# One Trainium2 kernel, four graph blocks: three pieces of work change places on ScalarE and VectorE

## The chip, the cores and the metric

The kernel runs on one core of a Trainium2 chip. Its time is the device time of one execution in microseconds; the kernel before takes 1280.2 us as the median of three runs (1279.27 to 1281.15). Less is better. The engines are TensorE (PE in the profile, its weight loads PEld), VectorE (DVE), ScalarE (ACT), GpSimd (POOL) and SyncE (SP), which here issues every DMA.

## The reference

For each of 32 graphs with 256 nodes and 256 features (`x`, a weighted adjacency `adj` 256x256, a node mask) four blocks follow each other, each added to its input and layer-normalized:

```python
x = _layernorm(x + _L0_gnn_ref(x, adj, L0_gnn_W))      # relu([x, adj @ x / deg] @ W.T)
x = _layernorm(x + _L1_gnn_ref(x, adj, W1, b1, W2, b2, W3, b3))  # three GCN layers
x = _layernorm(x + _L2_gnn_ref(x, nodemask, adj, adj, W_qkv, W_out, b_out))
x = _layernorm(x + _L3_gnn_ref(x, adj, W_qk, W_v))
```

The third block is attention with 8 heads of 64; the softmax is mixed with `adj` and `exp(-adj)` before it multiplies the values. The last block is a gate: `w = softmax over the nodes of sum(scores * adj)`, and its result is `w * v`. All of it is in float32.

## The kernel before

The kernel has no scheduler: for each engine the order of work is written out by hand as a list of calls, `first_graphs()`, then `slot(s)` in a loop (`FIRST, LAST = 5, G + 1`, 28 slots), then `last_graphs()`. Each engine runs its list strictly in that order; between engines there are only semaphores. A slot works on several graphs at once, each at another stage, so the numbers s - 2, s - 4, s - 6 in the calls are graphs. The same moment has another s on each engine (VectorE's s is ScalarE's s plus 2).

Most products are made of float32r parts: ScalarE copies a result out of PSUM as its high part (`..._h`, line 429), VectorE subtracts that from the result for the low part (`..._l`, line 900), and TensorE multiplies high by high and high by low in one stretch (HI) and low by high in a second (LO). So TensorE waits twice for each operand, for ScalarE and then for VectorE.

The work around the change, with the names of the profile:

- Attention runs over four pairs of heads. `scores(g, p, i)` (VectorE, line 1092) takes the scores of pair p out of PSUM, masks them and finds the row minimum; each call is two reductions. `exps` (ScalarE, line 578) makes the exponentials. `out_hi(g, p)` and `out_lo(g, p)` split a pair's output into `oT_h` and `oT_l`.
- `degrees(g)` on ScalarE (line 482) sums the rows of `adj`; VectorE uses the sums much later.
- The GCN: `gcn_out` (VectorE, line 1071) adds the third layer's product to `x1_b3`, giving `x2_pre`. Behind it `sup0_lo` makes the low part of the next graph's first product, for which TensorE waits in `aggregate(g, LO)` (line 1626, the product `psum<-sup_l,adjT_h`). Then come the normalization `norm_stats`, `norm_mean`, `norm_apply` and TensorE's `x2_transpose`.
- The gate: `tail_gate` makes `minus_gate`, a column of 256 numbers. SyncE turns it into a row by a DMA (`gate_row`); `gate_maximum`, `gate_exps` and `gate_probs` make the softmax on that row, and SyncE turns the row back into a column by a second DMA (`gate_col<-gate_prob`). `tail_out` (VectorE, line 1187) forms the gated sum `x4_pre = qkv3 * gate_col + x3` and waits for that DMA:

```python
if g < DMA_GATE:                                   # DMA_GATE = G - 3
    dve.wait_ge(dma_gate_col, 16 * once(g))
```

- SyncE's list, for k from 2 on, where `load(k)` issues xT, adjT, adj, x (256 KB each) and the mask row of graph k:

```python
if 0 <= k - 5 < DMA_GATE:
    turn_gate(k - 5)
if live(k):
    load(k)
if 0 <= k - 5 < DMA_GATE:
    turn_gate_probs(k - 5)
```

`load(k)` first waits until the buffers of graph k - 2 are free. The last of these in time is ScalarE's `mask_bias(k - 2)` (`minus_big`, line 501). `turn_gate_probs` issues `gate_col<-gate_prob`.

Of the kernel before, what the change touches and what calls it, by code (L numbers as in the profile page):

```python
# [13 lines left out]
def graph_blocks_kernel(nc, x_d, adj_d, nodemask, xT_d, adjT_d, w0_d, w123_d, L1_b1, L1_b2, L1_b3, wqkv_d, wout_d,  # L14
# [22 lines left out]
    with ctx:  # L37
# [200 lines left out]
        def live(g):  # L238
            return 0 <= g < G

        def loaded(g):
            return 16 * (g // 2 + 1)
# [184 lines left out]
        def _(act):  # L427
            def copy(dst, src, scale=1.0):
                return nc.scalar.activation(dst, src, ACT.Copy, scale=scale)  # L429
# [34 lines left out]
            def x_hi(g):  # L464
                if not live(g):
                    return
                act.wait_ge(dma_xT[g % 2], loaded(g))
                copy(fT_of(g)[0][:, :, :], xT_sb[:, g % 2]).then_inc(act_xT, 1)
# [7 lines left out]
            def degrees(g):  # L476
                if not live(g):
                    return
                act.wait_ge(dma_adj[g % 2], loaded(g))
                reuse(act, dve_rdeg, once(g - 1))  # L480
                for t in range(NT):
                    last = nc.scalar.activation(adj_junk[:, t], adj_sb[:, g % 2, t], ACT.Copy,
                                                accum_out=deg[:, t:t + 1])
                last.then_inc(act_deg, 1)
# [104 lines left out]
            def out_hi(g, p):  # L589
                if not live(g):  # L590
                    return
                act.wait_ge(pe_pv, nth(g, p))
                copy(oT[0][:, p], bank(PV[p])[:, 0:N]).then_inc(act_oT, 1)
# [41 lines left out]
            def slot(s):  # L635
                probs_t(s - 3, 2, 0)
                probs_t(s - 3, 2, 1)
                hidden(0, s - 1)
                hidden_hi(0, s - 1)
                probs_t(s - 3, 3, 0)  # L640
                probs_t(s - 3, 3, 1)
                out_hi(s - 3, 2)
                x_hi(s)
                degrees(s)
                exps(s - 2, 0, 0)
                out_hi(s - 3, 3)
                sup_hi(1, s - 1)
                exps(s - 2, 0, 1)
                qk_hi(s - 2, 2)
                gate_exps(s - 4)  # L650
                exps(s - 2, 1, 0)
                hidden(1, s - 1)
                hidden_hi(1, s - 1)
                adj_exp(s)
                exps(s - 2, 1, 1)
                mask_bias(s - 1)
                adj_hi(s)
                norm_apply(3, s - 5)
                sup_hi(2, s - 1)
                sup0_hi(s)  # L660
                values(s - 2)
                self_copy(s)
                qk_hi(s - 2, 3)
                probs_t(s - 2, 0, 0)
                probs_t(s - 2, 0, 1)
                probs_t(s - 2, 1, 0)
                probs_t(s - 2, 1, 1)
                x2_hi(s - 1)
                norm_apply(2, s - 3)
                exps(s - 2, 2, 0)  # L670
                exps(s - 2, 2, 1)
                out_hi(s - 2, 0)
                x3_hi(s - 3)
                x1_hi(s)
                exps(s - 2, 3, 0)
                qk_hi(s - 1, 0)
                exps(s - 2, 3, 1)
                sup_hi(0, s)
                tail_qkv(s - 3)
                out_hi(s - 2, 1)  # L680
                qk_hi(s - 1, 1)
# [211 lines left out]
        def _(dve):  # L893
# [51 lines left out]
            def norm_mean(k, g):  # L945
                if not live(g):
                    return
                dve.wait_ge(dve_bn[k], once(g))
                for t in range(NT):
                    last = V_.bn_aggr(out=mv[:, k, t], in_=bn[:, k, t])  # L950
                last.then_inc(dve_mv[k], 1)
# [85 lines left out]
            def x1_bias(g):  # L1037
                if not live(g):
                    return
                if g == 0:  # L1040
                    dve.wait_ge(dma_biases, 16 * BIAS_DMAS)
                bias_sum(x1_b3[:, :, :], x1[:, :, :], b3_row).then_inc(dve_x1_b3, 1)
# [24 lines left out]
            def gcn_out(g):  # L1067
                if not live(g):
                    return
                dve.wait_ge(pe_gcn, once(g))  # L1070
                V_.tensor_tensor(x2_pre[:, :, :], halves(bank(GCN)), x1_b3[:, :, :], ALU.add) \
                    .then_inc(dve_x2_pre, 1)
# [13 lines left out]
            def scores(g, p, i):  # L1086
                if not live(g):
                    return
                dve.wait_ge(pe_scores, nth(g, p))
                dve.wait_ge(act_minus_big, once(g))  # L1090
                for h in range(2):
                    last = V_.tensor_tensor_reduce(  # L1092
                        out=prob[:, p % 2, i, h], in0=bank(SCORES[p] + h)[:, i * N:(i + 1) * N],
                        in1=minus_big[:, g % 2, i], scale=-QK_SCALE, scalar=3.0e38, op0=ALU.add, op1=ALU.min,
                        accum_out=shift[:, p % 2, h, i:i + 1])
                last.then_inc(dve_scores, 1)
# [8 lines left out]
            def probs(g, p, h):  # L1105
                if not live(g):
                    return
                if h == 0:
                    dve.wait_ge(dve_rsum, nth(g, p))
                for i in range(NT):  # L1110
                    last = V_.scalar_tensor_tensor(out=prob[:, p % 2, i, h], in0=prob[:, p % 2, i, h],  # L1111
                                                   scalar=rsum[:, p % 2, h, i:i + 1], in1=extra[:, g % 2, i],
                                                   op0=ALU.mult, op1=ALU.add)
                last.then_inc(dve_prob, 1)

            def out_lo(g, p):
                if not live(g):
                    return
                dve.wait_ge(act_oT, nth(g, p))
                lo(oT[1][:, p], bank(PV[p])[:, 0:N], oT[0][:, p]).then_inc(dve_oT, 1)  # L1120
# [71 lines left out]
            def slot(s):  # L1192
                scores(s - 4, 0, 0)
                hidden_lo(0, s - 3)
                scores(s - 4, 0, 1)
                out_lo(s - 5, 2)
                x1_bias(s - 3)
                out_lo(s - 5, 3)
                scores(s - 4, 1, 0)
                sup_lo(1, s - 3)  # L1200
                x_lo(s - 2)
                gate_maximum(s - 6)
                scores(s - 4, 1, 1)
                recip_sums(s - 4, 0)
                qk_lo(s - 4, 2)
                probs(s - 4, 0, 0)
                probs(s - 4, 0, 1)
                degrees(s - 2)
                hidden_lo(1, s - 3)
                gate_probs(s - 6)  # L1210
                adj_sum(s - 2)
                recip_sums(s - 4, 1)
                probs(s - 4, 1, 0)
                attention_out(s - 5)
                adj_lo(s - 2)
                sup_lo(2, s - 3)
                norm_stats(2, s - 5)
                probs(s - 4, 1, 1)
                gcn_out(s - 3)
                sup0_lo(s - 2)  # L1220
                norm_mean(2, s - 5)
                norm_stats(1, s - 3)
                norm_mean(1, s - 3)
                aggregate(s - 2)
                relu_residual(s - 2)
                norm_apply(1, s - 3)
                qk_lo(s - 4, 3)
                tail_out(s - 6)
                norm_stats(0, s - 2)
                norm_mean(0, s - 2)  # L1230
                scores(s - 4, 2, 0)
                scores(s - 4, 2, 1)
                x2_lo(s - 3)
                norm_apply(0, s - 2)
                scores(s - 4, 3, 0)
                scores(s - 4, 3, 1)
                norm_stats(3, s - 6)
                x3_lo(s - 5)
                out_lo(s - 4, 0)
                recip_sums(s - 4, 2)  # L1240
                x1_lo(s - 2)
                probs(s - 4, 2, 0)
                qk_lo(s - 3, 0)
                probs(s - 4, 2, 1)
                recip_sums(s - 4, 3)
                tail_k(s - 5)
                sup_lo(0, s - 2)
                out_lo(s - 4, 1)
                norm_mean(3, s - 6)
                probs(s - 4, 3, 0)  # L1250
                probs(s - 4, 3, 1)
                x2_bias(s - 3)
                qk_lo(s - 3, 1)
                tail_gate(s - 5)
                adj_extra(s - 2)
# [920 lines left out]
```

## Time and profile before

| | |
|---|---|
| median of three runs | 1280.2 us (1279.27 to 1281.15) |
| the profiled execution | 1280.6 us, of which span from first to last instruction 1278.7 us |
| busy, share of the span | PE 98%, PEld 90%, DVE 90%, ACT 75%, POOL 14% |
| chain that ended last | PE 94%, DVE 2%, ACT 2%, DMA 1% |
| DMA | mean 38 GB/s |

Matmuls are pipelined and their ends are modelled, so a start-to-start distance says more than a duration. On VectorE and ScalarE an instruction begins a little before the one ahead of it is recorded as ended. A number in brackets behind a row is the engine's idle time ahead of it, and what ended that.

### The profile page before, as it was taken

Reading aid. Unit: us, or ns where it says so; the run is one execution under the profiler, and the core shown is the slowest. Engines: PE = TensorE matmul, PEld = TensorE weight load, DVE = VectorE, ACT = ScalarE, POOL = GpSimd, SP = SyncE. Lnnn points to the kernel's source line nnn. Section 1 sums busy time; section 2 is a strip of 40 time slices with the busy share of each in tenths; the row PEclk is TensorE's granted clock in tenths of the full one; section 3 lists DMA queues with packets and bytes.
Section 4 is the critical chain, followed back from the end, with each engine's and each line's share of the span. In section 5 each row is a group of like instructions: output and inputs, shape, how many; then the busy total and the mean of one; then the engine's idle time right before and its main releaser. Section 6 shows DMA issues by size and latency. Waiting matters only on the chain.

```text
span 1278.7 us, 30231 instructions
## 1 busy us (share of the span) xinstructions
PE 1259.2 (98%) x10732; PEld 1156.0 (90%) x10732; DVE 1155.8 (90%) x3671; ACT 958.4 (75%) x2534; POOL 177.2 (14%) x383
## 2 busy tenths in 40 slices
PE   8999999999999999999999999999999999999997
PEld 7888999999999999999999999999999999999886
DVE  6988999999999999999999999999999999998895
ACT  6677678778778787777787787787787787787773
POOL 0001111101111101111111111011111011111011
PEclk9999999999999999999999999999999999999999
DMA  6110111110111100111100111101111101110000
GB/s 230 35 35 2 35 43 44 44 31 14 44 43 44 43 27 19 43 44 43 44 12 34 43 44 44 43 2 43 44 43 44 43 2 44 43 44 10 10 9 25
DMA packets 42659, 49.06 MB, mean 38 GB/s; under 512 B 16272, under 2 KB 25232, under 8 KB 42512
## 3 DMA queue, kind: packets, MB, share of 16 engines
q1 hardware_dynamic: 42512, 47.14, 11.7%
q8 instruction: 87, 1.43, 0.5%
q14 instruction: 60, 0.49, 0.1%
HBM read 38.68 MB, written 8.39 MB: 37 GB/s over the span
## 4 chain that ended last, share of the span: by engine, by line
PE 94%; DVE 2%; ACT 2%; DMA 1%; issue 1%; POOL 0%; SPq 0%; POOLq 0%; DVEq 0%
PE psum L1551 63%; PE psum L1565 11%; PE psum L1803 9%; PE psum L1761 8%; PE psum L1854 1%; PE psum L1857 1%; ACT work L578 1%; DMA adjT_sb<-in_adjT 0%; DVE bn L929 0%; DMA v_sb<-in_w 0%; DVE x L963 0%; DVE x_pre L1021 0%; POOL rstd L382 0%; DVE x_pre L1187 0%; DVE work L1092 0%
## 5 line engine op out<-in xcount | busy, mean ns | idle before, releaser
L578 ACT ACTIVATE work<-work,shift 128x256 f32<-128x256 f32 x512 | 253.7, 500 | 4.9 <-DVE shift L1092 4.8
L1111 DVE SCALAR_TENSOR_TENSOR work<-work,rsum,extra 128x256 f32<-128x256 f32 x512 | 216.8, 475 | 1.0
L1092 DVE CUSTOM_DVE_ANT_0 work<-psum,minus_big 128x256 f32<-128x256 f32 x512 | 189.0, 417 | 3.0 <-PE psum L1761 2.8
L429 ACT ACTIVATE work<-psum 128x512 f32<-128x512 f32 x256 | 138.0, 598 | 71.6 <-PE psum L1565 71.5
L379 POOL TENSOR_TENSOR mv<-mv,eps 128x2 f32<-128x2 f32 x128 | 31.0, 242 | 1081.7 <-DVE mv L950 1081.7
L1551 PE MATMUL psum<-x2T_h,wqkv_h 128*128 128x256 f32 x512 | 145.6, 284 | 0.0
L429 ACT ACTIVATE sup_h<-psum 128x512 fp32r<-128x512 f32 x124 | 73.2, 590 | 95.2 <-PE psum L1551 95.1
L1551 PE MATMUL psum<-x2T_h,wqkv_l 128*128 128x256 f32 x512 | 143.0, 279 | 0.0
L1551 PE MATMUL psum<-x2T_l,wqkv_h 128*128 128x256 f32 x512 | 142.9, 279 | 0.0
L1565 PE MATMUL psum<-ident,work 128*128 128x128 f32 x1024 | 127.4, 273 | 0.0
L1803 PE MATMUL psum<-work,v_sb 128*64 128x256 f32 x1024 | 124.6, 385 | 0.0
L429 ACT ACTIVATE qkT_h<-psum 128x512 fp32r<-128x512 f32 x128 | 75.8, 593 | 56.6 <-PE psum L1551 56.4
L1565 PEld LDWEIGHTS psum<-ident,work 128*128 128x128 f32 x1024 | 114.1, 141 | 1.0 <-DVE work L1111 0.6
L382 POOL TENSOR_TENSOR rstd<-mv,minus_half 128x2 f32<-128x2 f32 x128 | 106.9, 835 | 10.0
L1803 PEld LDWEIGHTS psum<-work,v_sb 128*64 128x64 f32 x1024 | 68.0, 136 | 36.2 <-issue 0.4
L900 DVE TENSOR_TENSOR oT_l<-psum,oT_h 128x256 fp32r<-128x256 f32 (+1 forms) x132 | 56.4, 428 | 46.9 <-ACT oT_h L429 44.8
L578 ACT ACTIVATION_READ_ACCUMULATOR work<-work,shift 128x1 f32 x512 | 98.4, 192 | 0.0
L1551 PEld LDWEIGHTS psum<-x2T_h,wqkv_h 128*128 128x128 f32 x512 | 96.6, 189 | 0.4 <-DVE x2T_l L900 0.2
L1551 PEld LDWEIGHTS psum<-x2T_l,wqkv_h 128*128 128x128 f32 x512 | 96.6, 189 | 0.0
L1551 PEld LDWEIGHTS psum<-x2T_h,wqkv_l 128*128 128x128 f32 x512 | 96.3, 188 | 0.0
L900 DVE TENSOR_TENSOR sup_l<-psum,sup_h 128x512 fp32r<-128x512 f32 x124 | 85.3, 688 | 11.0 <-ACT sup_h L429 11.0
L929 DVE BATCH_NORM_STATS2 bn<-x_pre 128x6 f32<-128x256 f32 x256 | 94.9, 414 | 0.3
(189 smaller groups left out, 3798.5 us busy)
## 6 DMA issues: line engine op xcount, KB each, us to landing
xT_sb<-in_xT SPq DMA_DIRECT2D x32, 256.0 KB, 2.6
adjT_sb<-in_adjT SPq DMA_DIRECT2D x32, 256.0 KB, 3.0
adj_sb<-in_adj SPq DMA_DIRECT2D x32, 256.0 KB, 4.0
x_sb<-in_x SPq DMA_DIRECT2D x32, 256.0 KB, 4.3
out<-y_sb SPq DMA_DIRECT2D x32, 256.0 KB, 3.5
work<-in_wqkv SPq DMA_DIRECT2D x1, 1536.0 KB, 9.6
mask_row<-in_nodemask SPq DMA_DIRECT2D x32, 32.0 KB, 4.2
w_raw<-in_w SPq DMA_DIRECT2D x3, 256.0 KB, 5.4
```

The costliest lines, as they stand in the source:

```text
L379: nc.gpsimd.tensor_tensor(mv[:, k, :, 1], mv[:, k, :, 1], eps[:, :], ALU.add) \
L382: nc.gpsimd.tensor_tensor(rstd[:, k], mv[:, k, :, 1], minus_half[:, :], ALU.pow) \
L429: return nc.scalar.activation(dst, src, ACT.Copy, scale=scale)
L578: last = nc.scalar.activation(prob[:, p % 2, i, h], prob[:, p % 2, i, h], ACT.Exp, bias=shift[:, p % 2, h, i:i + 1], scale=-1.0, accum_out ...
L900: return V_.tensor_tensor(dst, src, f32(hi_part), ALU.subtract)
L929: last = V_.bn_stats(out=bn[:, k, t], in_=src[:, t])
L1092: last = V_.tensor_tensor_reduce(out=prob[:, p % 2, i, h], in0=bank(SCORES[p] + h)[:, i * N:(i + 1) * N], in1=minus_big[:, g % 2, i], scal ...
L1111: last = V_.scalar_tensor_tensor(out=prob[:, p % 2, i, h], in0=prob[:, p % 2, i, h], scalar=rsum[:, p % 2, h, i:i + 1], in1=extra[:, g % 2 ...
L1551: last = mm(dst, left, right, start=opens and n == 0, stop=closes and n == len(steps) - 1)
L1565: last = nc.tensor.transpose(dst[:, r * N + t * P:r * N + (t + 1) * P], src[:, t, block_of(r)], ident[:, :])
L1761: last = mm(bank(SCORES[p] + h)[:, i * N:(i + 1) * N], qkT[left][rows, p % 2, 0, block_of(i)], qkT[right][rows, p % 2, 1], start=n == 0 an ...
L1803: last = mm(bank(PV[p])[h * D:(h + 1) * D, 0:N], v_sb[:, k, (2 * p + h) * D:(2 * p + h + 1) * D], probT[:, p % 2, h, k], start=k == 0, sto ...
```

## The change

Only the order of three calls is another; no instruction is added or taken away, and TensorE's, GpSimd's and SyncE's lists are the same.

```diff
 # ScalarE, slot(s)
                 x_hi(s)
+                out_hi(s - 3, 3)
                 degrees(s)
                 exps(s - 2, 0, 0)
-                out_hi(s - 3, 3)
                 sup_hi(1, s - 1)
...
 # VectorE, slot(s)
                 x1_bias(s - 3)
+                scores(s - 4, 1, 0)
+                scores(s - 4, 1, 1)
                 out_lo(s - 5, 3)
-                scores(s - 4, 1, 0)
                 sup_lo(1, s - 3)
                 x_lo(s - 2)
                 gate_maximum(s - 6)
-                scores(s - 4, 1, 1)
...
                 probs(s - 4, 1, 1)
+                tail_out(s - 6)
+                norm_mean(2, s - 5)
                 gcn_out(s - 3)
                 sup0_lo(s - 2)
-                norm_mean(2, s - 5)
                 norm_stats(1, s - 3)
...
                 qk_lo(s - 4, 3)
-                tail_out(s - 6)
                 norm_stats(0, s - 2)
```

VectorE in the second half of a slot, from the probabilities of pair 1 (L1111) on, before. L1071 is `gcn_out`, the `sup_l` row behind it `sup0_lo`, the first L950 `norm_mean(2)`, L1187 `tail_out`; in brackets the semaphores that each waits for:

```order
L1111 SCALAR_TENSOR_TENSOR work<-work,rsum,extra 128x256 x2
L1071 TENSOR_TENSOR x_pre<-psum,x_b 128x512 [waits pe_gcn]
L900 TENSOR_TENSOR sup_l<-psum,sup_h 128x512 [waits act_sup0]
L950 BN_AGGR mv<-bn 128x2 [waits dve_bn_2]
L950 BN_AGGR mv<-bn 128x2
L929 BN_STATS bn<-x_pre 128x6 [waits dve_x2_pre]
...
L900 TENSOR_TENSOR qkT_l<-psum,qkT_h 128x2x256 [waits act_qk]
L1187 SCALAR_TENSOR_TENSOR x_pre<-qkv,gate_col,x 128x256 [waits act_x3,act_y,dma_gate_col]
L1187 SCALAR_TENSOR_TENSOR x_pre<-qkv,gate_col,x 128x256
```

The same place of the changed kernel:

```order
L1111 SCALAR_TENSOR_TENSOR work<-work,rsum,extra 128x256 x2
L1187 SCALAR_TENSOR_TENSOR x_pre<-qkv,gate_col,x 128x256 [waits act_x3,act_y,dma_gate_col]
L1187 SCALAR_TENSOR_TENSOR x_pre<-qkv,gate_col,x 128x256
L950 BN_AGGR mv<-bn 128x2 [waits dve_bn_2]
L950 BN_AGGR mv<-bn 128x2
L1071 TENSOR_TENSOR x_pre<-psum,x_b 128x512 [waits pe_gcn]
L900 TENSOR_TENSOR sup_l<-psum,sup_h 128x512 [waits act_sup0]
L929 BN_STATS bn<-x_pre 128x6 [waits dve_x2_pre]
```

The gated sum, with its wait for the DMA, and the mean of the third normalization stand ahead of the GCN's output and of `sup_l`; they stood behind them.

VectorE in the first half of the slot, before: `x1_bias` (L1035), `out_lo` of pair 3 (`oT_l`), the first and, behind `gate_shift`, the second score step of pair 1 (L1092, the rows with waits):

```order
L1035 TENSOR_TENSOR x_b<-x,b_row 128x512
L900 TENSOR_TENSOR oT_l<-psum,oT_h 128x256 [waits act_oT]
L1092 ISA work,shift<-psum,minus_big 128x256 [waits act_minus_big,pe_scores]
...
L900 TENSOR_TENSOR sup_l<-psum,sup_h 128x512 [waits act_sup_1]
L900 TENSOR_TENSOR fT_l<-xT_sb,fT_h 128x512 [waits act_xT]
L1161 TENSOR_REDUCE gate_shift<-gate_row 1x1 [waits dma_gate_row]
L1092 ISA work,shift<-psum,minus_big 128x256 [waits act_minus_big,pe_scores]
...
L1103 RECIPROCAL rsum<-psum_exp 128x4 [waits act_exp]
```

The same place of the changed kernel:

```order
L1035 TENSOR_TENSOR x_b<-x,b_row 128x512
L1092 ISA work,shift<-psum,minus_big 128x256 [waits act_minus_big,pe_scores]
...
L1092 ISA work,shift<-psum,minus_big 128x256 [waits act_minus_big,pe_scores]
...
L900 TENSOR_TENSOR oT_l<-psum,oT_h 128x256 [waits act_oT]
L900 TENSOR_TENSOR sup_l<-psum,sup_h 128x512 [waits act_sup_1]
L900 TENSOR_TENSOR fT_l<-xT_sb,fT_h 128x512 [waits act_xT]
L1161 TENSOR_REDUCE gate_shift<-gate_row 1x1 [waits dma_gate_row]
L1103 RECIPROCAL rsum<-psum_exp 128x4 [waits act_exp]
```

Both score steps stand ahead of the low half now, and `gate_shift` has one score step less between it and what follows. SyncE's list is untouched: the four loads and the mask row of one graph stand ahead of `gate_col<-gate_prob` in both kernels; what changed is the place in VectorE's list at which that DMA is waited for.

## Rows read from the trace of the kernel before

**Rows 1.** The page: its first line, and the chain by engine.

```profile
span 1278.7 us, 30231 instructions
...
PE 94%; DVE 2%; ACT 2%; DMA 1%; issue 1%; POOL 0%; SPq 0%; POOLq 0%; DVEq 0%
```

**Rows 2.** TensorE's waits from 111 to 1193 us: total, times, longest us.

```profile
PE psum L1551 <- DVE shift L1092: 0.2, 1, 0.2
```

**Rows 3.** Timeline of TensorE in one slot: start us, us, instruction.

```profile
636.59 0.63 PE L1551 MATMUL psum<-sup_l,adjT_h 128*128 128x256 f32 x4
...
646.20 0.41 PE L1551 MATMUL psum<-w_h,x3T_h 128*128 128x384 f32 x1
646.45 0.34 PE L1551 MATMUL psum<-w_l,x3T_h 128*128 128x384 f32 x1
646.63 0.34 PE L1551 MATMUL psum<-w_h,x3T_h 128*128 128x384 f32 x1
```

**Rows 4.** Timeline of VectorE in the same slot; in brackets idle time ahead.

```profile
622.49 0.42 DVE L900 TENSOR_TENSOR oT_l<-psum,oT_h 128x256 fp32r<-128x256 f32 x1 [1.54 <-ACT oT_h L429]
...
624.11 0.68 DVE L900 TENSOR_TENSOR fT_l<-xT_sb,fT_h 128x512 fp32r<-128x512 f32 x1
624.71 0.40 DVE L1161 TENSOR_REDUCE gate_shift<-gate_row 1x1 f32<-1x256 f32 x1
...
634.89 0.69 DVE L1071 TENSOR_TENSOR x_pre<-psum,x_b 128x512 f32<-128x512 f32 x1 [0.33 <-PE psum L1551]
635.52 0.69 DVE L900 TENSOR_TENSOR sup_l<-psum,sup_h 128x512 fp32r<-128x512 f32 x1
636.13 0.24 DVE L950 BATCH_NORM_AGGREGATE mv<-bn 128x2 f32<-128x6 f32 x2
636.28 0.72 DVE L929 BATCH_NORM_STATS2 bn<-x_pre 128x6 f32<-128x256 f32 x2
...
640.26 0.87 DVE L1187 SCALAR_TENSOR_TENSOR x_pre<-qkv,gate_col,x 128x256 f32<-128x256 f32 x2
641.05 0.75 DVE L929 BATCH_NORM_STATS2 bn<-x_pre 128x6 f32<-128x256 f32 x2
```

**Rows 5.** Timeline of ScalarE in the same slot.

```profile
622.35 0.58 ACT L429 ACTIVATE sup_h<-psum 128x512 fp32r<-128x512 f32 x1
...
625.14 0.51 ACT L612 ACTIVATE gate_exp<-gate_row,gate_shift 1x256 f32<-1x256 f32 x1 [0.74 <-DVE gate_shift L1161]
...
629.51 0.89 ACT L501 ACTIVATE minus_big<-mask_row,big_col 128x256 f32<-128x256 uint8 x2
```

**Rows 6.** Timeline of SyncE's DMA issues in the same slot.

```profile
630.49 0.33 SPq L272 DMA_DIRECT2D xT_sb<-in_xT  x1
...
632.82 0.49 SPq L313 DMA_DIRECT2D gate_col<-gate_prob  x1
```

**Rows 7.** DMA issues from 616 to 618, 630 to 634, 130.9 to 134: KB, us to landing.

```profile
gate_row<-minus_gate SPq DMA_DIRECT2D x1, 1.0 KB, 1.9
...
gate_col<-gate_prob SPq DMA_DIRECT2D x1, 1.0 KB, 3.2
...
gate_col<-gate_prob SPq DMA_DIRECT2D x1, 1.0 KB, 3.4
```

**Rows 8.** The tile gate_col on SyncE, 160 to 1140 us, 26 issues.

```profile
DMA to landing us min/median/max: 2.9/3.7/5.4
```

**Rows 9.** Timeline of the first slot with a gated sum, all engines.

```profile
133.31 0.55 SPq L313 DMA_DIRECT2D gate_col<-gate_prob  x1
...
134.58 0.74 PE L1551 MATMUL psum<-sup_l,adjT_h 128*128 128x256 f32 x4
```

**Rows 10.** The page: group of the score reductions; busy us, mean ns of one.

```profile
L1092 DVE CUSTOM_DVE_ANT_0 work<-psum,minus_big 128x256 f32<-128x256 f32 x512 | 189.0, 417 | 3.0 <-PE psum L1761 2.8
```

**Rows 11.** Two stretches at the end: PE, PEld, DVE, ACT, POOL busy (x), clock, DMA.

```profile
1262.00:1274.00 12.00, 7.75 (x54) 6.69 (x54) 6.38 (x24) 2.14 (x5) 0.88 (x2) 1.00 0.06 22
1274.50:1278.70 4.20, 0.00 (x0) 0.00 (x0) 0.73 (x2) 0.00 (x0) 0.61 (x1) 0.50 0.18 62
```

## The prediction, made before the changed kernel ran

> **What bounds the kernel now.** I read the page first: the chain that ended last is 94% TensorE [rows 1]. Then TensorE's waits over the 28 slots, from 111 to 1193 us: one idle stretch of 0.2 us in all [rows 2]. So in a slot the matmuls follow each other at their own pace, and the other engines only have to be in time. An edit on ScalarE or VectorE can then take very little away, but it can add a wait on every slot if it makes an operand late. What is left to win is hidden in start-to-start distances: the first matmul of the last block's projection (L1551, `w_h,x3T_h`) is followed after 0.25 us, the next after 0.18 [rows 3], so 0.07 us a slot go there, where TensorE's list waits for VectorE's last scores and ScalarE's `x3T_h`.
>
> Next the timelines of VectorE, ScalarE and SyncE in one slot. VectorE waits 1.54 us for `oT_h` of pair 3 and 0.33 us for the GCN's product ahead of `gcn_out` (L1071) [rows 4]; ScalarE waits 0.74 us for `gate_shift` [rows 5]. These are the waits that the change goes for. None of them is on TensorE's path.
>
> **The change part by part.** *Pair 3's output and pair 1's scores.* ScalarE's copy moves ahead of the degrees; the degrees come a copy later, and VectorE uses them only much later in the slot, so that costs nothing. VectorE does the two score steps in its 1.54 us of waiting [rows 4]: four reductions of at most 0.42 us [rows 10], 1.67 us, so the low half of pair 3 begins between 1.54 - 1.67 = 0.13 us later and a little earlier than before. TensorE shows no wait near its use [rows 2], so zero. VectorE then waits for `sup_h`, which ends at 622.35 + 0.58 = 622.93 [rows 5]; two low halves of 0.60 us each (624.71 - 624.11) [rows 4] bring `gate_shift` to about 624.16 instead of 624.71, 0.55 us earlier at best, at worst not earlier. I take 0.5, since only a wait for TensorE ahead of the moved copy stands against it. ScalarE's wait for `gate_shift` shrinks by as much, and `minus_big`, which ends at 629.51 + 0.89 = 630.40 [rows 5], comes 0.5 us earlier too. That matters, because SyncE's load of the next graph is issued right behind it, at 630.49 [rows 6].
>
> *The gated sum ahead of the GCN's output.* This is the step on which the time hangs. `tail_out` needs the gate's column. SyncE issues that DMA behind the loads of one graph, at 632.82 [rows 6], and it lands 3.2 us later [rows 7], at 636.02. Before, VectorE came to `tail_out` at 640.26 [rows 4] and found it there. Now it comes to it at the latest where it used to come to `gcn_out`, at 634.89 - 0.33 = 634.56 [rows 4]. The column, 0.5 us earlier by the part above, lands at 635.52. VectorE runs its list in order, so `gcn_out`, `sup0_lo` and all behind them stand still with it, and TensorE waits for `sup0_lo`.
>
> Step by step for this slot [rows 3, 4]: `tail_out` begins at 635.52 + 0.05 = 635.57 (0.05 for the semaphore, my estimate from how close waiting instructions follow in these timelines). It takes 641.05 - 640.26 = 0.79, and `norm_mean` 636.28 - 636.13 = 0.15. So `gcn_out` begins at 636.51 instead of 634.89. `sup0_lo` begins 635.52 - 634.89 = 0.63 later and takes 0.69: done at 637.83. TensorE's low stretch of the aggregate begins 0.06 later, at 637.89, instead of 636.59. That is a stall of 1.30 us. Before, `sup0_lo` ended at 635.52 + 0.69 = 636.21, only 0.38 us ahead of its use, so there is little cover to lose. What comes next, the normalization and `x2_transpose`, hangs on the same `gcn_out` and moves with TensorE, so I add nothing for it; `norm_mean` stands no longer between, which gives it 0.15 back.
>
> This slot is one of the good ones. Over 26 issues the column takes 2.9 to 5.4 us to land, median 3.7 [rows 8]. The spread reaches further up than down and the issue itself is sometimes late, so I take 3.85 for the mean, 0.65 more than here: 1.95 us a slot, 26 x 1.95 = 50.7 us. In the first slot with a gated sum the column is issued at 133.31 [rows 9] and lands after 3.4 [rows 7], at 136.71. I give it no earlier load, since ScalarE's list there is still that of the first graphs, which the change leaves alone. TensorE would go on at 136.71 + 0.05 + 0.79 + 0.15 + 0.63 + 0.69 + 0.06 = 139.08 instead of 134.58 [rows 9]: 4.5 us. In the last graphs nothing is moved.
>
> Is it certain that the column lands so late? The row of the turned row, the same 1 KB with nothing in front of it, says 1.9 us [rows 7]; the column behind four 256 KB loads takes 3.2 and more. The Trainium skill, "DMA: Bandwidth & Descriptors", section "Anatomy of one DMA — SWDGE (gpsimd) path", gives a DMA about 2.0 us plus its bytes over 436 GB/s; that is fitted on another path than SyncE's, and for 1 KB it would be 2.0 us, a sum near that of the third case below. The trace agrees for the row alone and not for the column behind the loads, so the measured landings decide.
>
> *What is given back.* `tail_out` no longer stands between `gcn_out` and the later scores. VectorE reaches the last scores earlier, and the 0.07 us ahead of the projection can go [rows 3]: 27 x 0.07 = 1.9 us, at worst nothing.
>
> **Sum.** 50.7 + 4.5 - 1.9 = 53.3 us on the profiled execution's 1280.6 us (1278.7 of it span [rows 1]): 1333.9, say 1334. The median of the runs is 0.4 lower, which I leave inside the range.
>
> **The rivals.**
>
> *The clock falls.* TensorE idles in every slot for about 2 us, once for 4.5. Near the end of the trace it was busy for 7.75 of 12 us and still had its full clock of 2.4 GHz; in the stretch without any matmul the record says 0.50, the level of 1.2 GHz [rows 11]. The Trainium skill, "TensorE: Matmul & The Clock Gate", "Part 1: The HAM clock gate", says that an idle TensorE is throttled to half and that activity releases it. For this rival speak the long stalls (5.4 - 3.2 = 2.2 us more than in the slot above gives 3.5 us, and the first one); against it that most are much shorter than the pause at the end. At half speed each microsecond of matmul costs half a microsecond more. If 27 stalls each brought 1 us of that, it is 13.5 us: 1347. Two or three long ones alone give some 5 us.
>
> *The column lands as soon as a lone transfer does.* That would hold if the loads did not delay it: issued at 632.32, landed 1.9 later [rows 7] at 634.22. VectorE would find it there at 634.56, and only the moved work itself would delay `gcn_out`: 634.56 + 0.79 + 0.15 = 635.50, 0.61 late, TensorE on at 636.88 instead of 636.59, 0.29 a slot. With the 0.07 back, 27 x 0.22 = 5.9 us: 1286.5; if VectorE also comes 0.4 us earlier, nothing is lost and it is 1279. Against it stand all 26 landings [rows 8].
>
> *Not slower at all.* The same wait would vanish if the loads were issued earlier: from the point at which the column lands at 633.9, that is 2.1 us before the row's 636.02, `gcn_out` is not late and only the 1.9 us of the projection are left: 1278.7. It needs `minus_big` 2.1 us earlier, and ScalarE has 0.74 us of waiting to give away ahead of it [rows 5], so little speaks for it.
>
> **How the numbers follow.** 82% for the forecast (1317 to 1350), 10% for the falling clock on top of it, 5% for the column alone, 3% for no wait at all. Bounds of the first: no earlier load adds 26 x 0.5 = 13 us, 1347; a load a further 0.4 us earlier takes 10, and the median 3.7 in place of 3.85 takes 4: 1320. With some room for the clock above and for landings below, 1316 to 1352. A measurement of this kernel can tell about 0.2%, 2.6 us, from no change. Faster by more than that: 0.02, the third rival with more given back than I see. Within it: 0.05, from the last two. Slower: 0.93.
>
> **What would show it.** In the profile of the changed kernel VectorE should wait ahead of L1187 for the DMA `gate_col`, one to three microseconds in 27 slots and some 50 us in all. TensorE should wait in 27 slots for VectorE's `sup_l` ahead of `psum<-sup_l,adjT_h`, at the same sum, and its busy share should fall by about 4 points. VectorE's wait for `oT_h` should shrink, ScalarE's wait for `gate_shift` to a third, and the load be issued about 0.5 us earlier against TensorE's products. The prediction is wrong if VectorE shows no wait at L1187 (then the column's landing was misread), if the stall is much larger than the column's lateness (then something behind `gcn_out` is late too), or if the granted clock falls inside the slots.

## The result, and the profile after

The changed kernel takes 1343.59 us (median of 4 runs, 1340.35 to 1345.5), the kernel before 1279.8 beside it: ratio 1.0494, 95% interval 1.0482 to 1.0507, so 4.9% slower. The profiled execution took 1344.06 us, 63.5 us more than that of before.

The page of the changed kernel, the span, the busy time and the chain that ended last:

```profile
span 1342.2 us, 30231 instructions
...
PE 1269.3 (95%) x10732; PEld 1164.7 (87%) x10732; DVE 1159.0 (86%) x3671; ACT 964.0 (72%) x2534; POOL 178.1 (13%) x383
...
PE 56%; ACT 17%; DVE 9%; DMA 8%; issue 5%; SPq 4%; POOL 0%; POOLq 0%; ACTq 0%; DVEq 0%
```

In [rows 1] the chain was 94% TensorE. Now it leaves TensorE in every slot, and runs through ScalarE, SyncE's queue, a DMA and VectorE. The waits of VectorE, TensorE and ScalarE from 100 to 1260 us say through which (line, releaser: us in total, times, longest):

```profile
DVE x_pre L1187 <- DMA gate_col<-gate_prob: 53.5, 27, 4.3
...
DVE oT_l L900 <- ACT oT_h L429: 2.6, 2, 1.8
```

```profile
PE psum L1551 <- DVE sup_l L900: 52.2, 27, 4.8
```

```profile
ACT gate_exp L612 <- DVE gate_shift L1161: 5.5, 26, 0.2
```

TensorE waited 0.2 us in all before [rows 2]; now it waits 27 times for `sup_l`, 52.2 us, and VectorE 27 times for the column. Of the small waits that the change goes for, the one for `oT_h` is gone but for two times, the one for `gate_shift` down to 5.5 us from 19.3 in the same stretch of before.

One slot as it now runs: SyncE's timeline from 742 us, then VectorE's from 746 and TensorE's from 748.9 (start, duration; in brackets the wait ahead of it):

```profile
742.62 0.34 SPq L272 DMA_DIRECT2D xT_sb<-in_xT  x1
...
744.95 0.49 SPq L313 DMA_DIRECT2D gate_col<-gate_prob  x1
```

```profile
746.10 0.86 DVE L1111 SCALAR_TENSOR_TENSOR work<-work,rsum,extra 128x256 f32<-128x256 f32 x2
749.07 0.88 DVE L1187 SCALAR_TENSOR_TENSOR x_pre<-qkv,gate_col,x 128x256 f32<-128x256 f32 x2 [2.10 <-DMA gate_col<-gate_prob]
749.87 0.24 DVE L950 BATCH_NORM_AGGREGATE mv<-bn 128x2 f32<-128x6 f32 x2
750.02 0.66 DVE L1071 TENSOR_TENSOR x_pre<-psum,x_b 128x512 f32<-128x512 f32 x1
750.60 0.68 DVE L900 TENSOR_TENSOR sup_l<-psum,sup_h 128x512 fp32r<-128x512 f32 x1
```

```profile
749.02 0.28 PE L1551 MATMUL psum<-sup_h,adjT_l 128*128 128x256 f32 x1
751.33 0.74 PE L1551 MATMUL psum<-sup_l,adjT_h 128*128 128x256 f32 x4 [2.04 <-DVE sup_l L900]
751.91 0.28 PE L1551 MATMUL psum<-x2T_h,wqkv_h 128*128 128x256 f32 x1
752.02 0.28 PE L1551 MATMUL psum<-x2T_l,wqkv_h 128*128 128x256 f32 x1
```

The column is issued 2.33 us behind the load (742.62 to 744.95) and lands 4.1 later. `tail_out` starts 0.02 us behind the landing; from its start it is 0.95 to `gcn_out` and 1.53 to `sup_l`, and TensorE goes on 0.05 after that one has ended. The reader sees one straight line from the DMA to TensorE with nothing to hide it: 2.10 us of waiting on VectorE are 2.04 on TensorE.

Behind some of these stalls the matmuls are further apart. TensorE's timeline in an earlier slot:

```profile
709.09 0.72 PE L1551 MATMUL psum<-sup_l,adjT_h 128*128 128x256 f32 x4 [2.16 <-DVE sup_l L900]
709.65 0.38 PE L1551 MATMUL psum<-x2T_h,wqkv_h 128*128 128x256 f32 x1
709.82 0.42 PE L1551 MATMUL psum<-x2T_l,wqkv_h 128*128 128x256 f32 x1
710.04 0.41 PE L1551 MATMUL psum<-x2T_h,wqkv_l 128*128 128x256 f32 x1
710.25 0.41 PE L1551 MATMUL psum<-x2T_h,wqkv_h 128*128 128x256 f32 x1
```

Two stretches that begin with the same product, the first behind that stall and the second behind the one shown before it (length, busy us and count of PE, PEld, DVE, ACT, POOL, granted clock, DMA):

```profile
709.80:712.80 3.00, 3.00 (x16) 3.00 (x15) 2.27 (x7) 0.39 (x1) 2.51 (x6) 0.50 0.00 0
751.90:753.10 1.20, 1.20 (x13) 1.20 (x12) 1.05 (x6) 0.00 (x0) 0.72 (x2) 1.00 0.00 0
```

Granted clock 0.50 is the level of 1.2 GHz. At it the matmuls start 0.21 us apart, at 2.4 GHz (1.00) 0.11. That comes in 7 of the 27 slots with a stall.

**The account.** From start to start the 27 slots are 64.4 us longer than before. Stalls (what TensorE idles ahead of `sup_l,adjT_h`, less the usual pitch of 0.12): 56.5, the first 4.96 and the other 26 in the mean 1.98. Twenty slots grew by 0.05 to 0.18 less than their stall, 0.117 in the mean: that is what is given back, 27 x 0.117 = 3.2. The seven slots with a stretch at 1.2 GHz grew by 10.2 us more than their stalls; with their share of what is given back, 7 x 0.117 = 0.8, the lower clock cost 11.0, or 1.6 each. 56.5 - 3.2 + 11.0 = 64.3. Ahead of and behind these slots 0.9 us are saved.

### The profile page after: what moved, and what is told of

Read it like the earlier page. It is cut to its first block, busy times and chain, and to the rows that moved or that the text cites. A ratio compares the mean times of both kernels' runs of the same rounds, so it can differ in the third digit from the quotient of the medians.

```text
span 1342.2 us, 30231 instructions
## 1 busy us (share of the span) xinstructions
PE 1269.3 (95%) x10732; PEld 1164.7 (87%) x10732; DVE 1159.0 (86%) x3671; ACT 964.0 (72%) x2534; POOL 178.1 (13%) x383
## 4 chain that ended last, share of the span: by engine, by line
PE 56%; ACT 17%; DVE 9%; DMA 8%; issue 5%; SPq 4%; POOL 0%; POOLq 0%; ACTq 0%; DVEq 0%
PE psum L1551 28%; PE psum L1565 11%; DMA gate_col<-gate_prob 8%; PE psum L1761 8%; PE psum L1803 7%; ACT work L578 6%; SPq L272 3%; ACT adj_junk L482 2%; DVE x_pre L1187 2%; ACT minus_big L501 2%; ACT hid L543 2%; DVE sup_l L900 1%; DVE fT_l L900 1%; DVE x_pre L1071 1%; ACT gate_exp L612 1%
## 5 line engine op out<-in xcount | busy, mean ns | idle before, releaser
L1111 DVE SCALAR_TENSOR_TENSOR work<-work,rsum,extra 128x256 f32<-128x256 f32 x512 | 216.6, 474 | 1.0
L1092 DVE CUSTOM_DVE_ANT_0 work<-psum,minus_big 128x256 f32<-128x256 f32 x512 | 188.2, 419 | 21.6 <-PE psum L1761 21.6
L379 POOL TENSOR_TENSOR mv<-mv,eps 128x2 f32<-128x2 f32 x128 | 39.9, 311 | 1144.5 <-DVE mv L950 1144.5
L1551 PE MATMUL psum<-x2T_h,wqkv_h 128*128 128x256 f32 x512 | 149.3, 292 | 0.0
L1551 PE MATMUL psum<-x2T_l,wqkv_h 128*128 128x256 f32 x512 | 146.3, 286 | 0.0
L1551 PE MATMUL psum<-x2T_h,wqkv_l 128*128 128x256 f32 x512 | 146.2, 286 | 0.0
L1551 PEld LDWEIGHTS psum<-x2T_l,wqkv_h 128*128 128x128 f32 x512 | 100.6, 196 | 0.0
L1551 PEld LDWEIGHTS psum<-x2T_h,wqkv_h 128*128 128x128 f32 x512 | 100.1, 195 | 0.4 <-DVE x2T_l L900 0.2
L1551 PEld LDWEIGHTS psum<-x2T_h,wqkv_l 128*128 128x128 f32 x512 | 100.0, 195 | 0.0
L382 POOL TENSOR_TENSOR rstd<-mv,minus_half 128x2 f32<-128x2 f32 x128 | 95.3, 745 | 10.0
L1551 PE MATMUL psum<-sup_l,adjT_h 128*128 128x256 f32 x248 | 44.3, 302 | 52.4 <-DVE sup_l L900 52.2
```

Source lines behind the costliest of these rows:

```text
L382: nc.gpsimd.tensor_tensor(rstd[:, k], mv[:, k, :, 1], minus_half[:, :], ALU.pow) \
L1092: last = V_.tensor_tensor_reduce(out=prob[:, p % 2, i, h], in0=bank(SCORES[p] + h)[:, i * N:(i + 1) * N], in1=minus_big[:, g % 2, i], scal ...
L1551: last = mm(dst, left, right, start=opens and n == 0, stop=closes and n == len(steps) - 1)
```

## The experiments

**One part at a time.** The kernel before with only the gated sum and the third mean moved ahead of `gcn_out`:

```diff
                 probs(s - 4, 1, 1)
+                tail_out(s - 6)
+                norm_mean(2, s - 5)
                 gcn_out(s - 3)
                 sup0_lo(s - 2)
-                norm_mean(2, s - 5)
                 norm_stats(1, s - 3)
...
                 qk_lo(s - 4, 3)
-                tail_out(s - 6)
```

> The kernel before with the gated sum and its mean alone ahead of the GCN's output; pair 3's copy and pair 1's scores stay where they were. My theory (VectorE stands at the gated sum until the gate's column lands, TensorE waits for the low part behind it): ScalarE keeps its 0.74 us of waiting, so the load and with it the column are not 0.45 us earlier; stalls of 1.98 + 0.45 = 2.43 us in 26 slots and about 5 us in the first, 68 us, less some 0.1 us a slot given back, plus more than 7 stretches at the lower clock of some 1.6 us each (10 to 14 of them): 1280 + 68 - 3 + 16 to 22 = 1361 to 1368 us, range 1352 to 1375. Rival (the three moves work together and the scores in the wait are what costs): this one alone is below the changed kernel, 1280 to 1320 us.

And only the other part, ScalarE's copy and the scores:

```diff
                 x_hi(s)
+                out_hi(s - 3, 3)
                 degrees(s)
                 exps(s - 2, 0, 0)
-                out_hi(s - 3, 3)
...
                 x1_bias(s - 3)
-                out_lo(s - 5, 3)
                 scores(s - 4, 1, 0)
+                scores(s - 4, 1, 1)
+                out_lo(s - 5, 3)
...
                 gate_maximum(s - 6)
-                scores(s - 4, 1, 1)
```

> The changed kernel with the gated sum and its mean back behind the GCN's output, that is the moves of pair 3's copy and pair 1's scores alone. My theory: these two remove waits of VectorE (1.54 us) and ScalarE (0.74 us) that no TensorE wait hangs on: 1277.5 to 1281 us, the load issued about 0.45 us earlier against the end of pair 3's product, the column with it. Rival (the two moves make an operand late and take part in the loss): 1290 us or more.

The first took 1355.26 us (ratio 1.0615, 1.0557 to 1.0673), the second 1279.14 (0.9996, 0.9987 to 1.0005). The waits of the first for the column, and for `oT_h` as before the change:

```profile
DVE x_pre L1187 <- DMA gate_col<-gate_prob: 56.9, 27, 3.1
DVE oT_l L900 <- ACT oT_h L429: 43.5, 29, 1.8
```

And those of the second:

```profile
DVE oT_l L900 <- ACT oT_h L429: 4.0, 4, 1.8
```

So the whole loss is in the gated sum. The first run lies in its expected range, 6 us below the 1361 to 1368 that were worked out; its four executions spread from 1350.72 to 1369.84, and the profiled one has nine stretches of lower clock in its slots, where 10 to 14 were expected. Without the other part the load is issued 10.19 us behind the end of pair 3's product, with it 9.74; the mean stall is 2.34 instead of 1.98. The other part alone takes 41 us of VectorE's waiting for `oT_h` (44.8 before, over the same stretch) and nothing measurable from the time: TensorE had no wait to lose, and VectorE waits for `sup_h` (28.4 us, 8.9 before) and `hidT_h` (16.4, 2.3 before) instead. Where the column hangs on the load, it is worth some 12 us (1355.26 to 1343.59).

**The column's place in SyncE's list.** The changed kernel with the column issued ahead of the load, and the kernel before with the same edit:

```diff
-                if live(k):
-                    load(k)
                 if 0 <= k - 5 < DMA_GATE:
                     turn_gate_probs(k - 5)
+                if live(k):
+                    load(k)
```

> The changed kernel with SyncE's list in another order: the gate's column is issued ahead of the next graph's loads. My theory (the column is late because it is issued and drained behind the loads): it is issued right behind the gate's softmax, lands some 2 us later, before VectorE comes to the gated sum; no wait there, no wait of TensorE for the low part, and the 0.1 us a slot that the changed kernel gives back elsewhere stays: 1276 to 1279 us. Rival 1 (the moved 0.94 us of VectorE work itself delays the GCN's output, whatever the column does): 0.29 us a slot, 1285 to 1288 us. Rival 2 (the column is slow for another reason than the loads): as the changed kernel, 1335 to 1345 us.

> The kernel before with one edit: SyncE issues the gate's column ahead of the next graph's loads. All three moves are left out. My theory (there nobody waits for the column, since the gated sum comes some 4 us after it has landed, and the loads wait for ScalarE's mask bias anyway): no difference, 1278.5 to 1281 us, distance from slot to slot 38.60 us as before. Rival (the earlier column, not the moves, is what makes the version with both a little faster than before): 1276 to 1278.5 us.

The changed kernel becomes 1278.02 us (0.9985, 0.9976 to 0.9994), the kernel before 1280.42 (1.0003, 0.9994 to 1.0012). In the first, SyncE's timeline in one slot, and the column's landings over all:

```profile
627.90 0.49 SPq L313 DMA_DIRECT2D gate_col<-gate_prob  x1
629.10 0.33 SPq L272 DMA_DIRECT2D xT_sb<-in_xT  x1
```

```profile
DMA to landing us min/median/max: 1.9/1.9/2.5
```

VectorE has no wait at L1187 any more, and TensorE none of a slot's size. The column's turn was ready 1.2 us ahead of the load and had stood behind it in SyncE's list for nothing: first for the load's own waits, then behind its transfers. With the column out of the way the order that cost 64 us costs nothing. This version is the fastest of all measured here, by 0.15% of the kernel before: the interval is just off 1, and the size is below the 0.2% that the prediction gave a measurement to tell. The trace points the same way: all slots but the first and the last of the 27 are 38.50 to 38.57 us long, where before most are 38.56 to 38.65. The kernel before with the column first is not faster, so the earlier column alone is not what brings this.

A version between the two issues the column behind xT, adjT and adj, ahead of x and the mask row:

```diff
-            def load(g):
+            def load(g, column=-1):
...
                 load_x(g)
-                load_rest(g)
+                load_adjT(g)
+                load_adj(g)
+                if 0 <= column < DMA_GATE:
+                    turn_gate_probs(column)
+                load_nodes(g)
...
                 if live(k):
-                    load(k)
-                if 0 <= k - 5 < DMA_GATE:
+                    load(k, column=k - 5)
+                elif 0 <= k - 5 < DMA_GATE:
                     turn_gate_probs(k - 5)
```

> The changed kernel with the gate's column issued between the next graph's loads, behind xT, adjT and adj and ahead of x and the mask row. My theory (the column is late by what is issued and drained ahead of it): it is issued about 1.3 us behind the first load instead of 2.4 and lands 4.4 to 4.8 us behind it instead of 6.2, so the mean stall falls from 1.98 to about 0.4 us a slot with a few longer ones, and no or one stretch of the lower clock: 1283 to 1296 us. Rival (what counts is how much is in flight at the time, whatever the order of the issues): 1330 to 1345 us.

It took 1296.72 us (1.0141, 1.0117 to 1.0166), a little above the expected range. The profiled execution, 1303.96, is the slowest of its four, so its rows show somewhat more waiting than the median has. The column's landings, and VectorE's wait for them (L1191 is `tail_out`, four lines lower here):

```profile
DMA to landing us min/median/max: 1.9/3.3/5.7
```

```profile
DVE x_pre L1191 <- DMA gate_col<-gate_prob: 16.9, 22, 3.1
```

Fewer loads ahead bring it earlier, but not steadily. The 1.9 is the last column of these, which has no load ahead of it; behind three loads it is 2.5 to 4.0, and once 5.7. The mean stall of the 26 slots behind the first is 0.63 us instead of the 0.4 expected, and two stretches of lower clock came where none or one was expected. The issue itself came earlier too, so this run does not divide the gain between the two. The Trainium skill, "DMA: Bandwidth & Descriptors", section "Queues, rings and completion order", says that each DMA engine consumes the descriptors of a ring in their order, which SyncE's DMAs share; by that rule a 1 KB transfer issued last waits for what its engine still has to move. The landings agree (medians: 1.9 in front, 3.3 behind three, 3.6 behind all); the rings themselves no run here shows.

**How far the sum may be moved.** The gated sum behind `gcn_out` and `sup0_lo`, the rest as changed:

```diff
-                tail_out(s - 6)
                 norm_mean(2, s - 5)
                 gcn_out(s - 3)
                 sup0_lo(s - 2)
+                tail_out(s - 6)
```

> The changed kernel with the gated sum one step later, behind the GCN's output and the low half that TensorE waits for, but still ahead of the second normalization. My theory (the low half is what TensorE waits for first; the normalization and the transposition of x2 have next to no cover either): no wait of TensorE for the low half any more, but the normalization begins about 0.9 us later, so TensorE waits some 0.8 us a slot for x2 in the transposition, 3 us in the first: 1294 to 1306 us, with few or no stretches of the lower clock. Rival 1 (only the low half matters): 1277 to 1281 us. Rival 2 (the gated sum costs the whole lateness of the column wherever it stands ahead of the normalization): 1325 to 1345 us.

1300.89 us (1.0162, 1.0148 to 1.0176). TensorE's waits:

```profile
PE psum L1565 <- DVE x L963: 19.4, 27, 3.4
```

The wait for `sup_l` is gone, and the next thing is late: `x`, which TensorE transposes. A slot loses 0.7 us there (19.4 / 27) where it lost 1.9 for `sup_l` (52.2 / 27). Two things stand behind this. VectorE comes to the gated sum later, and in 16 of 27 slots the column is there by then; its wait:

```profile
DVE x_pre L1187 <- DMA gate_col<-gate_prob: 8.6, 11, 2.9
```

That is 8.6 us in place of 53.5. And in the slots without this wait TensorE still idles for `x`, 0.32 us in the one from 625.75 us, since the sum's own work now stands between `sup0_lo` and the normalization. So both the place in the list at which the column is waited for and what stands behind it set the price; this run does not divide the two further.

**What the clock costs.** First the changed kernel with 12 products that nobody reads, on TensorE ahead of the low stretch:

```diff
                 aggregate(s - 1, HI)
+                pe.wait_ge(dve_x3_pre, once(s - 4))
+                keep_busy(4, 12)
                 aggregate(s - 1, LO)
```

> The changed kernel with 12 transposes of the identity into a free PSUM bank between the high and the low stretch of the aggregate, in every slot: 1.3 us of TensorE work that is shorter than each stall, so it only fills idle time. Theory of the clock (seven stretches of 3.4 us at half clock cost about 1.6 us each, and they come from the idle time): the idle time shrinks to about 0.7 us a slot, at most one or two stretches are left (first slot, longest landing), 1344 - 8 to 11.5 = 1332 to 1336 us. Rival (the lower clock costs nothing beside the stalls, or does not come from them): 1342 to 1346 us with as many stretches.

1340.61 us (1.0471, 1.0451 to 1.0491), well above the expected range. In the profiled execution, with 1343.38 the slowest of its four, two stretches of lower clock remained in the slots instead of seven, but VectorE's wait for the column grew too:

```profile
DVE x_pre L1187 <- DMA gate_col<-gate_prob: 59.0, 27, 4.4
```

5.5 us more than in the changed kernel: the column was issued 2.60 us behind the load in the mean, instead of 2.43. Why, this run does not say. A stall that hangs on a DMA is no fixed quantity to test the clock with, so the next pair makes one without a DMA: the version with the column in front, and six reductions of constant rows ahead of `gcn_out`, once alone and once with the same 12 products:

```diff
+        scrap = sb("scrap", [P, 6, 6])
...
+            def spend():
+                for n in range(6):
+                    V_.bn_stats(out=scrap[:, n], in_=(b3_row, bout_row)[n % 2][:, :])
...
                 norm_mean(2, s - 5)
+                spend()
                 gcn_out(s - 3)
```

> The kernel with the column issued ahead of the load (1278.0 us, no wait at all), plus six reductions of constant rows (operation of line 929, into a buffer that nobody reads) ahead of gcn_out in each of the 28 slots: a stall of fixed length that no DMA has a part in. This output is the reference's. gcn_out comes about 6 x 0.36 = 2.2 us later, TensorE waits about 1.8 to 2.1 us for sup_l: 28 x 2 = 50 to 59 us. Theory (the idle time of TensorE is what lets its clock fall, in some slots, at about 1.6 us each): 5 to 9 stretches of lower granted clock in the slots, 8 to 14 us, so 1338 to 1350, and the sum of the time over that of the kernel without the reductions is larger than the sum of the stalls by these. Rival (the seven stretches have to do with the DMA that is late, not with idle time): no stretch, 1328 to 1337.

> The same, and TensorE runs 12 products that nobody reads, behind the third block's last pre-activation, so that it is busy for most of the stall. The stalls themselves have the same cause and the same length. Theory: no stretch or one or two of lower clock, granted clock 0.997 or more in the mean, and 7 to 12 us less than the run without them: 1330 to 1339. Rival (the lower clock costs nothing, or idle time has no part in it): as long as the run without them within 3 us, or longer by what the added products overrun the stall.

The first took 1347.57 us (1.0525, 1.0509 to 1.054), the second 1335.19 (1.0425, 1.0408 to 1.0443), both inside what their theory expected. TensorE's wait for `sup_l` in each (L1558 is the same line, seven lower):

```profile
PE psum L1558 <- DVE sup_l L902: 49.3, 27, 2.3
```

```profile
PE psum L1558 <- DVE sup_l L902: 13.9, 27, 1.0
```

Two neighbouring slots of the first, TensorE's timeline; each has one of these stalls:

```profile
301.89 0.81 PE L1558 MATMUL psum<-sup_l,adjT_h 128*128 128x256 f32 x4 [1.81 <-DVE sup_l L902]
302.50 0.42 PE L1558 MATMUL psum<-x2T_h,wqkv_h 128*128 128x256 f32 x1
302.71 0.42 PE L1558 MATMUL psum<-x2T_l,wqkv_h 128*128 128x256 f32 x1
...
343.94 0.74 PE L1558 MATMUL psum<-sup_l,adjT_h 128*128 128x256 f32 x4 [1.81 <-DVE sup_l L902]
344.51 0.28 PE L1558 MATMUL psum<-x2T_h,wqkv_h 128*128 128x256 f32 x1
344.63 0.28 PE L1558 MATMUL psum<-x2T_l,wqkv_h 128*128 128x256 f32 x1
```

Both idled 1.81 us; behind the first the matmuls are 0.21 us apart, behind the second 0.12. Nine slots of this run went like the first of these two. Eight of them are 42.03 to 42.06 us long from start to start, those without it 40.45 or 40.46: 1.59 us for each. (The ninth is the first slot, which is longer anyway.) With the added products every slot from the second on is 40.46 to 40.50 us until near the end, the clock falls in none of them, and the kernel is 12.4 us faster although TensorE does more work and VectorE's 2 us are the same. In the profiled executions the difference is 9.9: 13.2 us less in the 27 slots, 3.3 more ahead of and behind them, where one stretch of lower clock follows a stall that the products did not fill. (That stall of 2.10 us stands in the run without the products too, and there the clock stayed up.) So the idle time itself brings the lower clock, the late DMA has no part in it, and it costs 9 x 1.59 = 14 us here. The Trainium skill, "TensorE: Matmul & The Clock Gate", section "HAM oscillation — how this bites in real kernels", tells of a kernel whose DMA wait of about 3 to 5 us in every iteration brings the clock down in every iteration; here a shorter wait, 1.81 us, did so in one slot of three.

## Why the prediction was right, and what it missed

**Right in the place.** The gated sum waits for the column, `gcn_out` and `sup0_lo` wait behind it, and TensorE waits for `sup_l`: the rows after show each link, and taking the column out of its place in SyncE's list takes the whole loss away. That the other parts cost and bring nothing by themselves is shown too.

**Term by term.** The load came 0.45 us earlier, 0.5 was taken. The first stall was 4.96 (4.5), the others 1.98 in the mean (1.95); together 56.5 against 55.2, so these terms came out within 1.3 us. The estimate of 0.05 us for a semaphore was 0.02. Of the landing the prediction took 3.85 less 3.2, 0.65 above the slot that it worked out; the landings after are 3.2 to 5.3, median 3.6, and the mean is 3.78, so the spread carried over from before nearly unchanged.

**What is given back** was taken at 0.07 a slot, from TensorE's projection [rows 3]; it was 0.117, 3.2 us instead of 1.9. The version with the column in front gave the projection's 0.07 back, while with the scores and the copy alone the 0.25 of [rows 3] stays; so that part of the reason holds. The rest lies at two places that the prediction did not look at (start-to-start distances, medians over the slots without a lower clock): the transposition of `x2` gives back 0.12, its first two distances being 0.11 instead of 0.17, and the second product of `sup_l,adjT_h` takes 0.11, at 0.22 instead of 0.12. With the projection that is 0.09 of the 0.117; the reasons for these two were not tested.

**The step that failed** is the weighing of the clock. The forecast held it at full speed, and the case in which it falls was a rival at 10%, against which it was said "that most are much shorter than the pause at the end". The rows at the end showed one pause without any matmul and a stretch that was partly busy [rows 11], nothing in between, and so bore no statement on stalls of 2 us. The clock fell in 7 of 27 slots and cost 11.0 us, which is more than the 9.6 between 1334 and 1343.59; the other terms nearly cancel. A granted clock that falls inside the slots is one of the prediction's own signs of being wrong, and the time is nearer to that rival's 1347 than to the forecast's 1334. That it lies in the forecast's range (given as 1317 to 1350 and, a few lines on, as 1316 to 1352) is owed to the room left for the load and the landings, which came as forecast. The rival's 13.5 us was of the right size by another road: it took 1 us of half speed in each of 27 slots, where it was 3 us or more (the whole row of 709.80 above, 3.00 us, is at 0.50) in a quarter of them. That only the long stalls would do it is refuted: the seven are of 4.96, 2.31, 2.32, 3.41, 1.91, 2.04 and 2.14 us, while 2.37, 2.30 and 2.26 went by without. What decides which of equal stalls does it is left open here.

The other rivals are refuted. The column does not land like a lone transfer while it stands behind the load; it does as soon as it stands ahead, and then the time is that of the "not slower" case: 1278.0 where 1278.7 was worked out, by another way than the earlier load assumed there.

## What to carry to other kernels

Where an in-order engine waits for a DMA that can be late, everything behind it that the bounding engine needs is late too, so such a wait belongs behind it; before moving such a consumer up, look where the DMA stands in the issuing queue, since a small transfer there pays for what is ahead of it, and moving the issue may be all that the move needs. Idle time on VectorE or ScalarE while TensorE has no wait was worth nothing here: 41 us of one such wait went without a gain that could be measured. A stall that recurs costs more than its length: here a fifth on top, because the clock fell behind some of them, and where a stall can't be avoided, TensorE work that nobody reads can give most of that back. It did so behind the stall of fixed length (12.4 of 14 us); in the changed kernel itself, where the column came later as well, it gave 3 of 11.

## What was unexpected of the hardware

Of 27 stalls, all but the first of about 1.8 us, nine were followed by a stretch at 1.2 GHz (granted clock 0.50, matmuls 0.21 us apart instead of 0.11) that cost 1.59 us each, though the slots look alike; 12 unused products in the stall took all nine away, though one stretch then came ahead of these slots. And a 1 KB transfer issued behind three or four 256 KB ones on SyncE's queue landed after 2.5 to 5.7 us, in front of them mostly after 1.9 and at most after 3.6 (2.5 in the changed kernel).
